# Order of the first three shared products in a fused graph and mixture-of-experts layer

## The chip, the cores and the metric

The kernel runs on one core of a Trainium2 chip. The metric is the device time of one execution in microseconds; before the change it is 2880.34 us, the median of three runs (2879.47 to 2881.34).

The engines have these names: PE is TensorE (matrix products into PSUM banks), DVE is VectorE, ACT is ScalarE, POOL is GpSimd, SP is SyncE, which issues the loads of weights. They run their own programs side by side and wait for each other by semaphores.

## The reference

For 625 tokens of width 1024 the layer computes, in float32:

```
xn = layernorm(x)
x  = x + graph_attention(xn) + linear_attention(xn)
x  = x + ffn(layernorm(x))
ffn(t) = (silu(t @ sg) * (t @ su)) @ sd                    # shared, 1024 -> 8192 -> 1024
       + sum over the two chosen of 8 experts, at most 97 tokens each:
         w * (silu(g @ rg) * (g @ ru)) @ rd                # routed, 1024 -> 4096 -> 1024
```

The weights of the shared part (sg, su, sd) and of the experts (rg, ru, rd) are read once, about 500 MB.

## The kernel before

The graph and the attention parts take the first 470 us; then 32 steps of about 75 us do the feed-forward part. A step is an expert e (0 to 7) and a quarter q (0 to 3) of its inner width, and with it 256 columns of the shared inner width. Step 0 has an order of its own (`FIRST`), step 31 another (`LAST`); the 30 between them (`STEP`) run the code that is changed. In seven of these q is 0: there an expert begins, and its tokens, gathered from memory into `xg`, are transposed by PE (`turn_expert`), copied from PSUM by ACT (`tokens_hi`) and split by DVE (`tokens_lo`, which raises `xgT_ready`).

Weights arrive as 128x1024 blocks of float32 in a ring of raw buffers. Each block is used as a unit u: ACT casts it to a rounded high part (`hi(u)`, `c_hi`), DVE subtracts that from the block (`lo(u)`, `c_lo`), and PE forms each product of two numbers by three matmuls (`three`: high by high, high by low, low by high). High and low parts have a ring of seven places, and `hi(u)` waits until PE has used unit u-7. PE waits for `lo(u)` by `split(u)`.

The first seven units of a step serve the two shared up projections, gate and up, as a 2x2 block product done with seven products instead of eight. Their names are F_A11, F_S3, F_S2, F_A12, F_S1, F_A22, F_S4, for the units 0 to 6. Those with S take sums of raw blocks that DVE makes in place (`factor_sum`): S3 out of A11 and A21, then S2 out of S3, and so on. `product(j, i)` is the product i for the half j of the unit's columns, 12 matmuls into one PSUM bank; both halves use the same unit. The banks of half 0 are 2 to 5, those of half 1 are 6, 7, 0 and 1. Products with S3 and A11 start an empty bank; the later ones go on top of a copy of an earlier one, which ACT makes (`seed`). `keep_e7(j)` is ACT's copy of the S3 product out of its bank.

Bank 6 also gathers the routed down projection of the step before. So `product(1, F_A11)` waits for `rd_added`: ACT must first have copied this bank to `eout` (`routed_out(0)`), and it may do so only when PE is through with the last routed unit. In ACT's order, which is written out by hand, `routed_out(0)` stands behind `hi(3)`. The end of a step on PE is: the transposes of the second half of the routed inner rows (`turn_inner(1)`), then six units of `routed_down`, then the next step's `product(0, F_A11)`.

In the trace all matmuls of `three` have the lines L2164, L2167 and L2168. ACT: casts L736 (shared units) and L871, `routed_out` L960, seeds L890, `keep_e7` L895, tokens L972, `turned_hi` L915. DVE: low parts L1260 and L1630, sums for S3 L1243, S2 L1247, S1 L1250, S4 L1253, `turned_lo` L1739, `tokens_lo` L1745. PE's transposes are L2215 (`turn_inner`) and L2226 (`turn_expert`).

Of the kernel before, what the change touches and what calls it, by code (L numbers as in the profile page):

```python
# [103 lines left out]
F_A11, F_S3, F_S2, F_A12, F_S1, F_A22, F_S4 = range(NPROD)  # L104
# [64 lines left out]
def count(e, q, per_step, n):  # L169

    return e * (Q * per_step) + (q * per_step + n)
# [10 lines left out]
def build(nc, x, src, dst, W, a, w_qkv, w_out, b_out, router_w, rg, ru, rd, sg, su, sd, out):  # L182
# [3 lines left out]
    def sem(name):  # L186
        if name not in sems:
            sems[name] = ctx.enter_context(nc.semaphore(name))
        return sems[name]
# [280 lines left out]
    def raw_at_(q, b):  # L470

        return raw[(q * BLK + b) % RAW]

    def raw_sem(q, b):
        return sem(f"raw_in{(q * BLK + b) % RAW}")

    def raw_full(e, q, b):

        return e * (16 * Q * BLK // RAW) + 16 * ((q * BLK + b) // RAW + 1)
# [187 lines left out]
    def _(act):  # L667
# [57 lines left out]
        def factor_hi(e, q, order, i):  # L725
            u = order.at(i)
            r = order.raw(u)
            if SUM_BEFORE[i]:
                act.wait_ge(sem("sums"), count(e, q, 4, SUM_BEFORE[i]))
            else:  # L730
                act.wait_ge(raw_sem(q, r), raw_full(e, q, r))
            act.wait_ge(sem("unit_used"), count(e, q, U, u + 1 - RING + USED0))
            if order is FIRST and i in (F_A22, F_S4):
                act.wait_ge(sem("sums_y"), 4)
                act.wait_ge(sem("block_lo"), 2)
            nc.scalar.copy(c_hi[u % RING][:], raw_at_(q, r)[:]).then_inc(sem("hi_done"), 1)  # L736
# [66 lines left out]
        for n in range(2 * PAIRS):  # L803
            g, i = divmod(n, 4)
# [56 lines left out]
        def step(e, q, order=STEP):  # L861
            def hi(u):

                if order.shared(u):
                    return factor_hi(e, q, order, order.seq[u - order.s])
                r = order.raw(u)
                act.wait_ge(raw_sem(q, r), raw_full(e, q, r))
                act.wait_ge(sem("unit_used"), count(e, q, U, u + 1 - RING + USED0))
                if order is STEP and u in (order.sd + 2, order.sd + 3):
                    act.wait_ge(sem("down_sums"), count(e, q, 4, 2 * (u - order.sd - 1)))  # L870
                nc.scalar.copy(c_hi[u % RING][:], raw_at_(q, r)[:]).then_inc(  # L871
                    sem("hi_done"), 1 + (U - order.units) * (u == order.units - 1))
# [6 lines left out]
            def product_done(j, i):  # L879
                if j == 0:  # L880
                    act.wait_ge(sem("s_half"), count(e, q, NPROD, order.at(i) - order.s + 1))
                else:
                    act.wait_ge(sem("unit_used"), count(e, q, U, order.at(i) + 1 + USED0))
# [8 lines left out]
            def keep_e7(j):  # L892

                product_done(j, F_S3)
                nc.scalar.copy(s_up[:, j, 0:HW], PS[order.banks[j][3]][:, 0:HW]).then_inc(sem("seeded"), 1)  # L895
# [162 lines left out]
                tokens_hi(0)  # L1058
            hi(5)
            hi(6)  # L1060
            hi(7)
            keep_e7(0)
            if q == 0:
                tokens_hi(1)
            keep_e7(1)
# [54 lines left out]
        for q in range(Q):  # L1120
            step(0, q, FIRST if q == 0 else STEP)
        with act.Fori(1, E - 1) as e:
            for q in range(Q):
                step(e, q)
        for q in range(Q):
            step(E - 1, q, LAST if q == Q - 1 else STEP)
# [780 lines left out]
    def _(pe):  # L1907
# [132 lines left out]
        for n in range(2 * PAIRS):  # L2040
            g, i = G_Q + n // 4, n % 4
# [115 lines left out]
        def step(e, q, order=STEP):  # L2157
            def split(u):

                pe.wait_ge(sem("lo_done"), count(e, q, U, U + u + 1))  # L2160

            def three(out_, l_hi, l_lo, r_hi, r_lo, first, last, used=False, skip=False):

                m = MM(out_, l_hi, r_hi, start=first, stop=False, skip_group_check=skip)  # L2164
                if used:
                    m.then_inc(sem("unit_used"), used)
                MM(out_, l_hi, r_lo, start=False, stop=False, skip_group_check=skip)  # L2167
                return MM(out_, l_lo, r_hi, start=False, stop=last, skip_group_check=skip)  # L2168
# [16 lines left out]
            def product(j, i):  # L2185

                a, c, b, d = order.banks[j]
                bank = (a, d, a, b, a, c, d)
                after = {F_S2: TO_B, F_A12: TO_B, F_S1: TO_C, F_A22: TO_C, F_S4: TO_D}
                u = order.at(i)  # L2190
                t = FACTOR_TOK[i]
                split(u)
                if order is FIRST and j == 0:
                    pe.wait_ge(sem("block_lo"), BLK_LO.index(t) + 1)
                if i == F_S3 and order is FIRST:
                    pe.wait_ge(sem("silu_done"), count(e, q, 6, order.silus(1, 0)))
                elif i == F_S3 and j == 1 and order is LAST:
                    pe.wait_ge(sem("silu_done"), count(e, q, 6, order.silus(0, 1)))
                if i in after:
                    pe.wait_ge(sem("seeded"), count(e, q, 8, order.seeded(j, after[i])))  # L2200
                for k in range(4):
                    col = slice(k * 256 + j * P, k * 256 + (j + 1) * P)
                    m = three(PS[bank[i]][:, 0:HW], c_hi[u % RING][:, col], c_lo[u % RING][:, col],
                              tok_hi[t][:, k, :], tok_lo[t][:, k, :], k == 0 and i not in after, k == 3,
                              skip=(i in after))
                m.then_inc(sem("unit_used" if j else "s_half"), 1)
# [12 lines left out]
            def turn_expert(halves=(0, 1)):  # L2219

                pe.wait_ge(sem("xg_in"), e * 16 + 16)
                pe.wait_ge(sem("tlo_done"), count(e, q, 2, ONE))
                for half in halves:
                    for k in range(4):
                        c = (4 * half + k) * P
                        m = TR(PS[order.x_bank[half]][:, k * CAP:(k + 1) * CAP], xg[0:CAP, c:c + P], ident[0:CAP, 0:CAP])  # L2226
                    m.then_inc(sem("xgT_ps"), 1)
# [162 lines left out]
                return  # L2390

            product(0, F_A11)
            pe.wait_ge(sem("rd_added"), count(e, q, 2, 1))
            product(1, F_A11)
            if q == 0:
                turn_expert((0,))
                product(0, F_S3)
                product(0, F_S2)
                pe.wait_ge(sem("xgT_ready"), e * 2 + 1)
                turn_expert((1,))  # L2400
                product(0, F_A12)
                pe.wait_ge(sem("xgT_ready"), e * 2 + 2)
                for i in (F_S3, F_S2, F_A12):
                    product(1, i)
            else:
                for i in (F_S3, F_S2, F_A12):
                    product(0, i)
                    product(1, i)
            for i in (F_S1, F_A22, F_S4):
# [22 lines left out]
        for q in range(Q):  # L2432
            step(0, q, FIRST if q == 0 else STEP)
        for e in range(1, E - 1):
            for q in range(Q):
                step(e, q)
        for q in range(Q):
            step(E - 1, q, LAST if q == Q - 1 else STEP)
# [32 lines left out]
```

## Time and profile before

| what | value |
|---|---|
| median of three runs | 2880.34 us |
| profiled execution | 2882.55 us, of which the span is 2880.9 us |
| PE busy | 2801.1 us (97%) |
| DVE busy | 2364.3 us (82%) |
| ACT busy | 1783.4 us (62%) |
| mean granted clock of PE | 0.984 of full speed |
| mean DMA rate | 191 GB/s |

Busy time is the time in which at least one instruction of the engine runs. For PE it grows when the granted clock falls, so a busy PE isn't always a fast one. The clock has its own column in the views of single stretches.

### The profile page before, as it was taken

To read this page: it belongs to the slowest core of one execution; us is meant where nothing else is said; L and a number is where in the kernel's file an instruction comes from. 1 tells how busy PE (TensorE), PEld (TensorE's weight loads), DVE (VectorE), ACT (ScalarE), POOL (GpSimd) and SP (SyncE) were. 2 spreads that over 40 slices of the span, in tenths; PEclk is the share of its full clock that TensorE was granted. 3 is DMA by queue.
4 is the path that set the end of the run, shared out by engine and by line. 5 is a ranking of instruction groups with operands and counts; after the bars stand their busy time and mean duration, and the time that the engine had idled before them with its cause. 6 is when DMAs were issued, how large, how long until landed. Compare 5 with 4: busy or idle time off the path is not lost.

```text
span 2880.9 us, 42107 instructions
## 1 busy us (share of the span) xinstructions
PE 2801.1 (97%) x14756; PEld 2330.2 (81%) x14756; DVE 2364.3 (82%) x2957; ACT 1783.4 (62%) x2509; POOL 62.6 (2%) x74
## 2 busy tenths in 40 slices
PE   9999999999999999999999999999999999999998
PEld 8878898877777778887888877887888877777777
DVE  8857258988888888888888888888888888888888
ACT  7632224666666666666666666666666666666673
POOL 0010000000000000000000000000000000000001
PEclk9999999999999999999999999999999999999999
DMA  3011123766666666665666666667666666666676
GB/s 112 30 66 59 59 74 95 247 218 213 216 210 206 212 225 219 219 205 198 221 205 207 208 222 214 206 211 225 219 210 214 225 213 214 216 215 206 208 263 223
DMA packets 270286, 549.14 MB, mean 191 GB/s; under 512 B 16673, under 2 KB 82465, under 8 KB 269927
## 3 DMA queue, kind: packets, MB, share of 16 engines
q1 hardware_dynamic: 265954, 532.11, 56.2%
q0 software_dynamic: 3936, 14.06, 1.6%
q8 instruction: 118, 1.93, 0.3%
q14 instruction: 116, 0.95, 0.1%
q10 hardware_dynamic: 162, 0.08, 0.0%
HBM read 537.49 MB, written 8.70 MB: 190 GB/s over the span
## 4 chain that ended last, share of the span: by engine, by line
PE 78%; DVE 14%; issue 3%; ACT 3%; DMA 2%; ACTq 0%; SPq 0%; DVEq 0%
PE ps L2164 21%; PE ps L2167 21%; PE ps L2168 21%; DVE c_lo L1630 5%; PE ps L1928 3%; PE ps L1965 2%; PE ps L1967 2%; PE ps L1966 2%; DVE c_lo L1260 2%; ACT c_hi L736 1%; DVE raw L1247 1%; DVE raw L1243 1%; DMA raw<-in_L_ffn_su 1%; PE ps L2215 1%; PE ps L2056 1%
## 5 line engine op out<-in xcount | busy, mean ns | idle before, releaser
L1630 DVE TENSOR_TENSOR c_lo<-raw,c_hi 128x1024 fp32r<-128x1024 f32 x892 | 1055.4, 1219 | 246.3 <-ACT c_hi L871 245.3
L871 ACT CAST c_hi<-raw 128x1024 fp32r<-128x1024 f32 x892 | 903.3, 1048 | 226.0 <-PE ps L2168 83.0
L2164 PE MATMUL ps<-tok_hi,c_hi 128*128 128x314 f32 x1792 | 573.1, 320 | 62.9 <-ACT eout L960 62.5
L2168 PE MATMUL ps<-tok_hi,c_lo 128*128 128x314 f32 x1792 | 567.8, 317 | 0.0
L2167 PE MATMUL ps<-tok_lo,c_hi 128*128 128x314 f32 x1792 | 567.8, 317 | 0.0
L2164 PEld LDWEIGHTS ps<-tok_hi,c_hi 128*128 128x128 f32 x1792 | 353.7, 197 | 74.3 <-ACT eout L960 70.3
L2164 PE MATMUL ps<-c_hi,xgT_hi 128*97 128x512 f32 x1024 | 404.6, 395 | 0.0
L2168 PE MATMUL ps<-c_hi,xgT_lo 128*97 128x512 f32 x1024 | 403.1, 394 | 0.0
L2167 PE MATMUL ps<-c_lo,xgT_hi 128*97 128x512 f32 x1024 | 403.0, 394 | 0.0
L736 ACT CAST c_hi<-raw 128x1024 fp32r<-128x1024 f32 x224 | 228.7, 1049 | 215.0 <-DVE raw L1243 108.9
L2167 PEld LDWEIGHTS ps<-tok_lo,c_hi 128*128 128x128 f32 x1792 | 353.8, 197 | 1.4
L2168 PEld LDWEIGHTS ps<-tok_hi,c_lo 128*128 128x128 f32 x1792 | 352.8, 197 | 0.0
L1260 DVE TENSOR_TENSOR c_lo<-raw,c_hi 128x1024 fp32r<-128x1024 f32 x224 | 268.5, 1220 | 31.1 <-ACT c_hi L736 29.5
L2168 PEld LDWEIGHTS ps<-c_hi,xgT_lo 128*97 128x97 f32 x1024 | 166.1, 162 | 70.6
L2167 PEld LDWEIGHTS ps<-c_lo,xgT_hi 128*97 128x97 f32 x1024 | 166.3, 162 | 66.4
L2164 PEld LDWEIGHTS ps<-c_hi,xgT_hi 128*97 128x97 f32 x1024 | 166.3, 162 | 65.8
L2164 PE MATMUL ps<-c_hi,hT_hi 128*97 128x512 f32 x512 | 203.3, 397 | 0.0
L2168 PE MATMUL ps<-c_hi,hT_lo 128*97 128x512 f32 x512 | 201.6, 394 | 0.0
L2167 PE MATMUL ps<-c_lo,hT_hi 128*97 128x512 f32 x512 | 200.8, 392 | 0.0
L890 ACT COPY ps<-ps 128x314 f32<-128x314 f32 x192 | 78.8, 410 | 128.9 <-PE ps L2168 127.2
L1729 DVE TENSOR_TENSOR resid<-ps,resid 125x512 f32<-125x512 f32 x240 | 148.6, 681 | 0.0
L2164 PE MATMUL ps<-c_hi,sh_hi 128*125 128x512 f32 x340 | 134.4, 395 | 0.1
(286 smaller groups left out, 4083.7 us busy)
## 6 DMA issues: line engine op xcount, KB each, us to landing
raw<-in_L_ffn_rg SPq DMA_DIRECT2D x256, 512.0 KB, 5.0
raw<-in_L_ffn_ru SPq DMA_DIRECT2D x256, 512.0 KB, 4.1
raw<-in_L_ffn_rd SPq DMA_DIRECT2D x256, 512.0 KB, 5.0
raw<-in_L_ffn_sg SPq DMA_DIRECT2D x64, 512.0 KB, 5.9
raw<-in_L_ffn_su SPq DMA_DIRECT2D x64, 512.0 KB, 6.5
raw<-in_L_ffn_sd SPq DMA_DIRECT2D x64, 512.0 KB, 6.8
wl<-in_L_mix_w_qkv SPq DMA_DIRECT2D x6, 2048.0 KB, 8.0
wl<-in_L_gnn_W SPq DMA_DIRECT2D x2, 2048.0 KB, 21.9
```

Source lines behind the costliest of these rows:

```text
L736: nc.scalar.copy(c_hi[u % RING][:], raw_at_(q, r)[:]).then_inc(sem("hi_done"), 1)
L871: nc.scalar.copy(c_hi[u % RING][:], raw_at_(q, r)[:]).then_inc(sem("hi_done"), 1 + (U - order.units) * (u == order.units - 1))
L890: nc.scalar.copy(PS[to][:, 0:HW], PS[a][:, 0:HW]).then_inc(sem("seeded"), 1)
L1260: V.tensor_tensor(c_lo[u % RING][:], raw_at_(q, r)[:], c_hi[u % RING][:].bitcast(F32), ALU.subtract).then_inc(sem("lo_done"), 1)
L1630: V.tensor_tensor(c_lo[u % RING][:], raw_at_(q, r)[:], c_hi[u % RING][:].bitcast(F32), ALU.subtract).then_inc(sem("lo_done"), 1 + (U - ord ...
L1729: V.tensor_tensor(r, PS[bank][0:TP, :], r, ALU.add).then_inc(sem("sd_added"), n)
L1928: m = MM(PS[dt][0:TP, 0:SC], oh_d[slot(gr, c)][:, dt * TP:(dt + 1) * TP], oh_s[slot(gr, c)][:, 0:SC], start=(c == 0), stop=(c == EG - 1))
L1965: MM(ps, l_hi[:, k, ts], hi[:, i, :], start=(k == 0), stop=False)
L1966: MM(ps, l_hi[:, k, ts], lo[:, i, :], start=False, stop=False)
L2164: m = MM(out_, l_hi, r_hi, start=first, stop=False, skip_group_check=skip)
L2167: MM(out_, l_hi, r_lo, start=False, stop=False, skip_group_check=skip)
L2168: return MM(out_, l_lo, r_hi, start=False, stop=last, skip_group_check=skip)
```

## The change

PE: in every ordinary step `product(0, F_S3)` comes directly behind `product(0, F_A11)`, ahead of the wait for `rd_added` and of `product(1, F_A11)`. In the steps with q not 0 the sequence A11/0, A11/1, S3/0, S3/1, S2/0, ... becomes A11/0, S3/0, A11/1, S3/1, S2/0, ... In those with q=0 the sequence A11/0, A11/1, transposes, S3/0, S2/0, transposes, A12/0, S3/1, ... becomes A11/0, S3/0, A11/1, transposes, S2/0, transposes, A12/0, S3/1, ... ACT: `keep_e7(0)` goes ahead of `hi(7)` instead of behind it.

```diff
--- before.py
+++ after.py
@@ -1058,8 +1058,8 @@
                 tokens_hi(0)
             hi(5)
             hi(6)
+            keep_e7(0)
             hi(7)
-            keep_e7(0)
             if q == 0:
                 tokens_hi(1)
             keep_e7(1)
@@ -2390,11 +2390,11 @@
                 return
 
             product(0, F_A11)
+            product(0, F_S3)
             pe.wait_ge(sem("rd_added"), count(e, q, 2, 1))
             product(1, F_A11)
             if q == 0:
                 turn_expert((0,))
-                product(0, F_S3)
                 product(0, F_S2)
                 pe.wait_ge(sem("xgT_ready"), e * 2 + 1)
                 turn_expert((1,))
@@ -2403,7 +2403,8 @@
                 for i in (F_S3, F_S2, F_A12):
                     product(1, i)
             else:
-                for i in (F_S3, F_S2, F_A12):
+                product(1, F_S3)
+                for i in (F_S2, F_A12):
                     product(0, i)
                     product(1, i)
             for i in (F_S1, F_A22, F_S4):
```

## Rows read from the trace of the kernel before

**Rows 1.** The page: span, and busy time of each engine.

```profile
span 2880.9 us, 42107 instructions
...
PE 2801.1 (97%) x14756; PEld 2330.2 (81%) x14756; DVE 2364.3 (82%) x2957; ACT 1783.4 (62%) x2509; POOL 62.6 (2%) x74
```

**Rows 2.** Waits of PE: for whom, us in total, times, longest.

```profile
PE ps L2164 <- ACT eout L960: 62.5, 30, 3.2
...
PE ps L2164 <- DVE xgT_lo L1745: 0.4, 1, 0.4
```

**Rows 3.** PE timeline, step with q=2: start us, us, what [idle before].

```profile
1516.07 0.50 PE L2215 MATMUL ps<-ident,r_h 97*128 97x97 f32 x4
...
1524.71 0.31 PE L2164 MATMUL ps<-tok_hi,c_hi 128*128 128x314 f32 x1
...
1526.32 0.31 PE L2168 MATMUL ps<-tok_hi,c_lo 128*128 128x314 f32 x1
1528.61 0.42 PE L2164 MATMUL ps<-tok_hi,c_hi 128*128 128x314 f32 x1 [1.99 <-ACT eout L960]
```

**Rows 4.** Timeline of DVE, same stretch.

```profile
1517.12 0.56 DVE L1739 TENSOR_TENSOR hT_lo<-ps,hT_hi 128x388 fp32r<-128x388 f32 x1 [0.62 <-ACT hT_hi L915]
...
1521.01 1.22 DVE L1243 TENSOR_TENSOR raw<-raw,raw 128x1024 f32<-128x1024 f32 x1
1522.14 2.50 DVE L1260 TENSOR_TENSOR c_lo<-raw,c_hi 128x1024 fp32r<-128x1024 f32 x2
1524.75 1.23 DVE L1247 TENSOR_TENSOR raw<-raw,raw 128x1024 f32<-128x1024 f32 x1
```

**Rows 5.** Timeline of ACT, same stretch.

```profile
1526.08 1.99 ACT L736 CAST c_hi<-raw 128x1024 fp32r<-128x1024 f32 x2 [2.69 <-DVE raw L1247]
1527.98 1.07 ACT L960 COPY eout<-ps 97x512 f32<-97x512 f32 x2
1528.93 0.44 ACT L890 COPY ps<-ps 128x314 f32<-128x314 f32 x1
```

**Rows 6.** Stretches, PE alone: length, busy, PEclk (granted clock), DMA share, GB/s.

```profile
1526.62:1528.61 1.99, 0.00 (x2) 1.00 0.00 0
1529.37:1532.78 3.41, 3.41 (x15) 0.50 0.00 0
553.00:559.00 6.00, 5.60 (x37) 1.00 0.16 60
```

**Rows 7.** A11_1 to S1_0, q not 0, low clock: first of 17, sum.

```profile
702.12:715.96 13.84, 13.84 (x84) 0.88 0.59 204
...
sum 234.98, PE 234.97; mean PE 13.82
```

**Rows 8.** The same stretch in the five steps at full clock: one, sum.

```profile
1001.86:1014.14 12.28, 12.28 (x84) 1.00 0.58 186
...
sum 61.48, PE 61.47; mean PE 12.29
```

**Rows 9.** The same stretch in the seven steps with q=0: sum.

```profile
sum 105.43, PE 105.05; mean PE 15.01
```

**Rows 10.** Timeline of ACT in a step with q=0.

```profile
1979.76 1.05 ACT L736 CAST c_hi<-raw 128x1024 fp32r<-128x1024 f32 x1
...
1982.64 0.48 ACT L972 CAST xgT_hi<-ps 128x388 fp32r<-128x388 f32 x1 [0.24 <-PE ps L2226]
1983.02 2.00 ACT L736 CAST c_hi<-raw 128x1024 fp32r<-128x1024 f32 x2
```

**Rows 11.** Timeline of DVE in that step.

```profile
1984.11 1.22 DVE L1260 TENSOR_TENSOR c_lo<-raw,c_hi 128x1024 fp32r<-128x1024 f32 x1 [1.66 <-ACT c_hi L736]
1985.25 0.56 DVE L1745 TENSOR_TENSOR xgT_lo<-ps,xgT_hi 128x388 fp32r<-128x388 f32 x1
...
1987.99 0.56 DVE L1745 TENSOR_TENSOR xgT_lo<-ps,xgT_hi 128x388 fp32r<-128x388 f32 x1
```

**Rows 12.** One whole step at full clock, all engines.

```profile
629.03:702.12 73.09, 71.25 (x375) 58.49 (x375) 63.26 (x71) 49.70 (x69) 0.00 (x0) 1.00 0.65 216
```

## Prediction

> **What bounds the kernel now.** I read the page's head first: TensorE (PE) is busy for 2801.1 of 2880.9 us [rows 1], so its 80 us of idle time and the speed at which it runs are what there is to win. Second, the waits of PE: 62.5 us of the idle time are 30 waits of one kind, a matmul of a product that waits for ScalarE's copy of the routed accumulator into `eout` [rows 2]. Thirty is the number of ordinary steps, the one wait a step that `rd_added` makes. Third, the timelines around one such wait, in a step with q=2. PE turns the last routed rows at 1516.07, goes on without a pause to the last matmul of `product(0, F_A11)` at 1526.32, and starts `product(1, F_A11)` at 1528.61 after 1.99 us of idleness [rows 3]. VectorE (DVE) explains the lateness. After that turn it is fed at once (`hT_lo` at 1517.12, after 0.62 us of waiting for it) and then has no pause: three low parts, the sum for S3, the low parts of units 0 and 1 (until 1524.64), the sum for S2 (until 1525.98) [rows 4]. ScalarE takes `hi(2)` and `hi(3)` only when that sum is there (1526.08), and the copy to `eout` stands behind them: 1527.98 [rows 5]. So `product(1, F_A11)` starts 12.54 us after the turn whatever PE does in between, and PE has only 10.55 us of work for it.
>
> Fourth, the clock. During the 1.99 us the granted clock is still full; from 0.76 us after the restart it is 0.50 (1.2 of 2.4 GHz) for 3.41 us [rows 6]. The price is seen in the stretch from the start of `product(1, F_A11)` to the start of `product(0, F_S1)`. In the 17 steps with q not 0 and a clock below 1.00 it takes 234.98/17 = 13.82 us [rows 7], in the five with clock 1.00 it takes 61.48/5 = 12.30 [rows 8]. So a low stretch costs 1.52 us. In the seven steps with q=0, which hold two transposes of tokens besides, it takes 105.43/7 = 15.06, all at a lowered clock [rows 9].
>
> **The change, part by part.** Nothing is added or removed: the same matmuls, casts and DMAs, in another order on PE and, by one place, on ScalarE. No DMA issue is moved past anything.
>
> *`product(0, F_S3)` ahead of the wait.* Twelve matmuls from 1524.71 to 1526.32 give (1526.32-1524.71)/11 = 0.146 each, 1.75 a product [rows 3]. PE can issue the next product at 1526.47. Its unit is 1, whose low part is ready at 1524.64 [rows 4], 1.8 us before. It fills 1.75 us of idle time and leaves 1.99-1.75 = 0.24. It can't push the wait back: from the end of `lo(1)` to the restart there are 1528.61-1524.64 = 3.97 us, as the sum, two casts and the copy all follow on it, and the product needs 1.75, or 3.5 at half the clock. Its bank was last read by `turned_lo(1)`, which PE had to wait for before the fifth routed down unit. `product(1, F_A11)` therefore starts when it did, and every product behind it comes one product earlier.
>
> *The low clock.* It follows the idle time: the one step whose wait was only 0.40 us (at 555.95) shows clock 1.00 in the 6 us around it, 5.60 of them busy [rows 6]. With about 0.2 us left in the steps with q not 0, I take no low stretch there. That saves 1.52 more in 17 steps.
>
> The Trainium skill speaks against this term: "TensorE: Matmul & The Clock Gate", section "Why this matters for your kernels", warns only of idle gaps about as long as the longest of the 30 waits (3.2 us, rows 2). By that rule the low stretches would have another cause and stay; that is rival B. The trace does not agree, since 1.99 us are followed by 0.50 in rows 6.
>
> *Sum for q not 0.* The stretch falls to 12.30-1.75 = 10.55. Gain: 17 x (13.82-10.55) = 55.6; 5 x 1.75 = 8.8; in the step with the 0.40 us wait just 0.4. Together 64.8 us. Behind the stretch all is paced by PE: DVE waits for ScalarE's casts, these for ring places that PE frees, and so moves along. On the way nothing is late: after the restart ScalarE has four casts and four copies in front of `hi(8)`, about 4 x 1.0+4 x 0.42 = 5.7 us by the durations in rows 5, so the low parts of S1, A22 and S4 are there by about 7 us, and PE wants the first of them at 10.55. The seeds that S2 waits for are copied at 1528.93 (0.32 after the restart, [rows 5]) and when `product(1, F_A11)` has drained, some 2 us after it; PE comes to them 3.5 and 5.25 us after it.
>
> *Steps with q=0.* Here the transposes of the tokens have to be copied by ScalarE and split by DVE before `turn_expert((1,))` and `product(1, F_S3)` may start. Before, two products stood in front of the first of these waits, now one. I set `product(1, F_A11)` at 0 and take spacings of ScalarE and DVE from the step at 1979.09 [rows 10, 11]. `hi(4)` starts at 0.67 and takes 1.05; the seed of `product(1, F_A11)` starts when that product has drained, 1.95 (full clock), and takes 0.41; the transposes are over at 2.25; the copy of the first token half runs 2.30 to 2.78, `hi(5)` from 2.68, its low part from 3.77 (1.09 behind the cast's start, as at 1983.02 and 1984.11), `tokens_lo(0)` 4.91 to 5.47. PE has done with transposes and `product(0, F_S2)` at 3.77, so it waits about 1.75 us and turns the second half at 5.5. ScalarE copies that at 6.05 to 6.53, DVE splits it behind `lo(7)` at 7.65 to 8.2. PE reaches `product(1, F_S3)` at 7.55 and waits 0.7. Three products on, `product(0, F_S1)` starts at 13.5 instead of 15.06: 1.55 us, 7 x 1.55 = 10.9. The bounds: with no token wait at all it would be 6 products and 0.6 for transposes, 11.1, gain 28; with both token waits ending where they end now in rows 11 (DVE done at 1985.81 and 1988.55, so 6.7 and 9.5), 14.7, gain 2.5. A low stretch after the 1.75 us idleness costs 1.52, of which the second wait hides 0.7, so 0.8 a step, 5.6 in all. I take 10 us, near the walk by rows. Of the idle time ahead of `product(1, F_A11)` in these steps (up to 3.2) 1.75 go as well, but that is the same gain: the start is unchanged.
>
> *`keep_e7(0)` ahead of `hi(7)`.* The copy of 0.42 us comes before a cast whose low part PE needs over 10 us later: nothing. Without that cover it would be 0.42 x 30 = 13 us. What it waits for is ready earlier than now.
>
> **Sum.** 64.8+10 = 75 us. The profiled execution took 2882.55 (span 2880.9), 2.2 above the median of the runs, so 2807.6 by it and 2880.3-75 = 2805 against the median. I say 2806.
>
> **Rivals.**
> A, the forecast: both terms, 2800 to 2814 with the token steps' bounds that I believe. Chance 0.75.
> B, the low clock stays in the steps that have it, because something else lowers it or the token waits and 0.24 us still suffice. Then 22 x 1.75+0.4 = 39, token steps some 4: 43 us, 2837. For it: five steps have no low stretch although PE idled before them too, the one at 1001.86 among them [rows 8], so idleness alone doesn't decide. Against: no low stretch in the step with 0.40. Chance 0.12, partly so included.
> C, another engine sets the pace once PE is shorter: DVE is busy for 63.26 of 73.09 us of a step [rows 12] and has next to no pause before the turn. If 73.09 were its floor, only the clock comes back: 17 x 1.52 = 26 us, 2854. Against: the waits of 0.62 us just before `hT_lo` show it waiting for PE's work [rows 4]. Chance 0.07.
> D, slower: the token chain. PE's cover in front of it goes from two products to one; if the gather or ScalarE's queue is later than in my walk and each such wait brings a low stretch, the stretch in the seven steps takes 16.6 instead of 15.06, +11 us, 2891. It decides the sum only if the other 23 steps give under 0.5 us each, that is with C at its fullest. Chance 0.03.
> E, the change does nothing, as something in front of `product(0, F_S3)` holds it until ScalarE's copy: 2880. Chance 0.03.
>
> **How the numbers follow.** 2806 is A. The range, 2798 to 2840, holds A and B; C, D and E lie outside. A measurement of this kernel tells 0.2% (6 us) from no change. Faster is A, B and C, 0.94; same 0.03; slower 0.03.
>
> **What would show it.** Right: PE's waits for `eout` fall from 62.5 to about 12 us, about 0.2 each in steps with q not 0; clock 1.00 in the stretches of rows 7, and 10.55 us for each; a new wait for `xgT_lo` of some 1.7 and 0.7 us in seven steps; 12.5 us from the turn to `product(1, F_A11)` as before; 71.3 us a step. Wrong: a clock of 0.50 after each step's start, or waits of PE for `c_lo` behind the products (C).

## The result, and the profile after

The changed kernel takes 2810.02 us (median of four runs, 2807.42 to 2810.77) against 2880.84 us before: the ratio is 0.9751, 95% interval 0.9734 to 0.9767. The forecast was 2806, with 2798 to 2840 as its range.

The page of the changed kernel; its profiled execution took 2810.77 us.

```profile
span 2809.2 us, 42107 instructions
...
PE 2763.9 (98%) x14756; PEld 2290.7 (82%) x14756; DVE 2363.4 (84%) x2957; ACT 1779.7 (63%) x2509; POOL 61.5 (2%) x74
```

As many instructions, 71.8 us less than the profiled execution before. PE's busy time fell by 37.2 us (2801.1 to 2763.9, [rows 1]) although it does the same matmuls: that part is the clock. The rest, 34.5 of the 71.7 us by which the span is shorter, is idle time.

Waits of PE in the changed kernel (for whom: us in total, times, longest):

```profile
PE ps L2226 <- DVE xgT_lo L1745: 10.4, 7, 1.5
PE ps L2164 <- ACT eout L960: 10.3, 24, 1.4
...
PE ps L2164 <- DVE c_lo L1260: 4.0, 3, 2.1
PE ps L2164 <- DVE xgT_lo L1745: 2.9, 7, 0.4
```

The wait for `eout` is down from 62.5 to 10.3 us [rows 2]. The first row is new, as forecast: the second transposes of the tokens, seven times, 1.49 us each. The third wasn't in the forecast.

The same stretch of the same step as in [rows 3], on PE:

```profile
1487.07 0.50 PE L2215 MATMUL ps<-ident,r_h 97*128 97x97 f32 x4
...
1497.45 0.30 PE L2164 MATMUL ps<-tok_hi,c_hi 128*128 128x314 f32 x1
...
1499.61 0.41 PE L2164 MATMUL ps<-tok_hi,c_hi 128*128 128x314 f32 x1 [0.24 <-ACT eout L960]
```

Between the turn of the routed rows and the restart there are 12.54 us, as before. The second product now begins at 1497.45 and takes 1.75 us of the pause, of which 0.24 us is left.

What the restart waits for, on DVE (one row) and ACT (two rows), with the distances of [rows 4, 5]:

```profile
1495.74 1.22 DVE L1247 TENSOR_TENSOR raw<-raw,raw 128x1024 f32<-128x1024 f32 x1
...
1497.07 2.00 ACT L736 CAST c_hi<-raw 128x1024 fp32r<-128x1024 f32 x2 [2.69 <-DVE raw L1247]
1498.98 1.07 ACT L960 COPY eout<-ps 97x512 f32<-97x512 f32 x2
```

The sum for S2 ends at 1496.96, ScalarE takes `hi(2)` and `hi(3)` at 1497.07, and `eout` comes 1.91 us later, as before (1527.98-1526.08 = 1.90). PE's new order changes none of these distances.

The stretch from the second A11 product to the first S1 product, for the 17 steps of [rows 7] (the first, and their sum), the five of [rows 8] (sum) and the seven of [rows 9] (one, sum). Columns: from and to, length, PE busy, granted clock, DMA share, GB/s.

```profile
698.97:709.53 10.56, 10.56 (x72) 1.00 0.50 157
...
sum 179.54, PE 179.51; mean PE 10.56
...
sum 52.80, PE 52.80; mean PE 10.56
...
770.45:784.13 13.68, 11.78 (x80) 1.00 0.65 219
...
sum 95.79, PE 82.48; mean PE 11.78
```

The 17 take 10.56 us each instead of 13.82, the five 10.56 instead of 12.30, the seven 13.68 instead of 15.06. The clock is 1.00 in all 30 steps. That is 55.4+8.7+9.6 = 73.7 us.

In a step with q=0, the transposes of both token halves and `product(1, F_S3)` on PE:

```profile
1936.64 0.50 PE L2226 MATMUL ps<-ident,xg 97*128 97x97 f32 x4
...
1940.39 0.56 PE L2226 MATMUL ps<-ident,xg 97*128 97x97 f32 x4 [1.49 <-DVE xgT_lo L1745]
...
1943.12 0.41 PE L2164 MATMUL ps<-tok_hi,c_hi 128*128 128x314 f32 x1 [0.41 <-DVE xgT_lo L1745]
```

At the starts of the experts 2 to 6 something else is late: DVE's sum for S3 waits for its load for 2.99, 1.54, 2.94, 0.11 and 0.91 us (in the kernel before 1.33, 0, 1.01, 0.93 and 0.27). At e=4, SyncE's queue issues the rows on L543 below, the last of the old step's loads and then the first of the new one's; the sum waits for the first `su`:

```profile
1608.93 14.48 SPq L543 DMA_DIRECT2D raw<-in_L_ffn_rd  x8
1630.44 0.39 SPq L543 DMA_DIRECT2D raw<-in_L_ffn_sg  x1
1631.02 2.67 SPq L543 DMA_DIRECT2D raw<-in_L_ffn_su  x2
...
1637.97 1.22 DVE L1243 TENSOR_TENSOR raw<-raw,raw 128x1024 f32<-128x1024 f32 x1 [2.94 <-DMA raw<-in_L_ffn_su]
```

The restart of this step comes 15.56 us after the turn instead of 12.54. There, and most of all at e=2, PE has to wait for the low part of unit 0 too, the third row of its waits. This looks like the sign of rival C, but it is another thing: DVE has nothing to do there until the load has landed.

### The profile page after: what moved, and what is told of

It reads as the page before. It is cut to its first block, busy times and chain, and to the rows that moved or that the text cites. A ratio compares the mean times of both kernels' runs of the same rounds, so it can differ in the third digit from the quotient of the medians.

```text
span 2809.2 us, 42107 instructions
## 1 busy us (share of the span) xinstructions
PE 2763.9 (98%) x14756; PEld 2290.7 (82%) x14756; DVE 2363.4 (84%) x2957; ACT 1779.7 (63%) x2509; POOL 61.5 (2%) x74
## 4 chain that ended last, share of the span: by engine, by line
PE 76%; DVE 15%; issue 4%; ACT 3%; DMA 1%; ACTq 0%; SPq 0%; DVEq 0%
PE ps L2164 20%; PE ps L2168 20%; PE ps L2167 20%; DVE c_lo L1630 6%; PE ps L1928 3%; PE ps L1965 2%; PE ps L1967 2%; PE ps L1966 2%; DVE c_lo L1260 2%; ACT c_hi L736 2%; DVE raw L1247 1%; DVE raw L1243 1%; DMA raw<-in_L_ffn_su 1%; PE ps L2215 1%; PE ps L2056 1%
## 5 line engine op out<-in xcount | busy, mean ns | idle before, releaser
L2164 PE MATMUL ps<-tok_hi,c_hi 128*128 128x314 f32 x1792 | 556.8, 311 | 17.6 <-ACT eout L960 10.3
L2168 PE MATMUL ps<-tok_hi,c_lo 128*128 128x314 f32 x1792 | 551.6, 308 | 0.0
L2167 PE MATMUL ps<-tok_lo,c_hi 128*128 128x314 f32 x1792 | 551.4, 308 | 0.0
L2164 PEld LDWEIGHTS ps<-tok_hi,c_hi 128*128 128x128 f32 x1792 | 338.9, 189 | 30.0 <-ACT eout L960 18.1
L2167 PEld LDWEIGHTS ps<-tok_lo,c_hi 128*128 128x128 f32 x1792 | 339.3, 189 | 1.3
L2168 PEld LDWEIGHTS ps<-tok_hi,c_lo 128*128 128x128 f32 x1792 | 337.7, 188 | 0.0
L2168 PE MATMUL ps<-c_hi,sh_lo 128*125 128x512 f32 x340 | 134.1, 394 | 0.0
```

## The experiments

Each run was compared with runs of the kernel before on the same chip; there were three chips. The medians were 2878.19 us for the two halves of the change, the whole useless product and the written-out loop; 2877.49 for the half useless product, the early copy to `eout` by itself, the tokens' earlier path and all edits together; 2880.03 for the early copy on the changed kernel and the two runs on ScalarE's part. Ratios are to them, with 95% intervals. Where two runs come from different chips, their ratios are compared, not their times; the changed kernel has 0.9751 and, on the third chip, 0.9759.

### The two halves of the change by themselves

Edit of the first (q not 0 alone), on PE; ScalarE's swap is bound to `if q:` in the same way:

```diff
             product(0, F_A11)
-            product(0, F_S3)
+            if q:
+                product(0, F_S3)
             pe.wait_ge(sem("rd_added"), count(e, q, 2, 1))
...
                 turn_expert((0,))
+                product(0, F_S3)
                 product(0, F_S2)
```

> The new order on PE and ScalarE in the 23 ordinary steps with q not 0 alone; the seven with q=0 keep the old one. Theory (each half of the change acts on its own steps, through the product that covers the wait and through the clock): stretches of 10.56 us at clock 1.00 in the 23 steps, about 62 us less than before, near 2817 us, and low clock left in most of the seven steps with q=0. Rival (the low clock belongs to the kernel as a whole, or returns when only some steps are mended): low stretches of 3.41 us stay in steps with q not 0 too, gain about 39 us, near 2842.

Measured: 2814.8 us, ratio 0.9775 (0.9758 to 0.9791), 63.4 us less. Stretches of the 22 steps with q not 0 other than step 1 (sum), and of the first and the last of the seven with q=0:

```profile
sum 232.33, PE 232.31; mean PE 10.56
...
771.50:786.25 14.75, 14.75 (x93) 0.88 0.60 202
...
2523.96:2537.64 13.68, 13.31 (x92) 1.00 0.67 222
```

232.33/22 = 10.56 us, all at full clock. Six of the seven steps with q=0, which kept their order, still run at a lowered clock. The clock is a matter of the single step.

The other half binds the same edits to `if q == 0`.

> The new order in the seven steps with q=0 alone. Theory: stretch from the second A11 product to the first S1 product 13.68 us instead of 15.06, with new waits for the tokens of 1.5 and 0.4 us and clock 1.00 there; gain 7 x 1.4 = 10 us less up to 4 us that PE loses again at the starts of experts, so 2871 to 2875. Rival (the token waits cost what the product gives): no gain, 2880. The other 23 steps keep 13.8 us and their low clock.

Measured: 2868.76 us, ratio 0.9967 (0.9955 to 0.9980), 9.4 us less, as expected. One step with q=3, then one of the seven with q=0 and their sum:

```profile
702.22:716.03 13.81, 13.81 (x84) 0.88 0.61 210
...
776.95:790.64 13.69, 11.79 (x81) 1.00 0.65 220
...
sum 95.82, PE 82.53; mean PE 11.79
```

The seven take 95.82/7 = 13.69 us. Of the other 22 steps (without step 1) 17 have a low stretch and five don't, as in the kernel before, after the same pauses of 1.84 to 1.99 us; but they are not the same five, only the first is spared in both. The halves add up: 63.4+9.4 = 72.8 us, and 0.9775 x 0.9967 = 0.9743 against 0.9751.

### Useless work in the place of the wait

```diff
+            product(0, F_A11, done=False)
             product(0, F_A11)
             pe.wait_ge(sem("rd_added"), count(e, q, 2, 1))
```

With `done=False` the product raises no semaphore; the second one starts the bank afresh and gives the same values.

> The kernel before, in which PE forms the product A11 of half 0 twice in each ordinary step, the second time over the first, so that the wait is filled with useless work and no product is moved. Theory (the low clock comes from the idle time ahead of it): no low stretch, 12.30 us from A11 of half 1 to S1 in the 17 steps instead of 13.82, about 13.5 instead of 15.06 in the seven with q=0; gain 26+10 = 36 us, near 2844. Rival (something else lowers the clock, idleness does not matter): the low stretches stay, 2880 us.

Measured: 2847.69 us, ratio 0.9897 (0.9881 to 0.9914), 30.5 us less, where 36 were expected. Against the profiled execution of before, on which the 36 us rest, it is 35.5 us (2882.55 to 2847.07). The nine runs of the kernel before on this chip had a mean granted clock of 0.986 to 0.988, the profiled one 0.984, so fewer of their steps may have been slow; they left no trace that would show it. 360 matmuls are added and the kernel is faster. The 17 steps (one, sum), and the sum of the seven with q=0:

```profile
702.39:714.68 12.29, 12.29 (x85) 1.00 0.58 195
...
sum 209.29, PE 209.27; mean PE 12.31
...
sum 95.77, PE 93.18; mean PE 13.31
```

209.29/17 = 12.31 us at clock 1.00, where the kernel before has 13.82 at 0.88. The low clock comes from the idle time, and what it costs is 1.5 us a step. Rival B falls.

The Trainium skill, "TensorE: Matmul & The Clock Gate", section "Why this matters for your kernels", warns only of idle gaps over about 3 us. The trace does not agree: 18 of the 24 gaps that lowered the clock in the kernel before were 1.84 to 1.99 us.

The last row says something that the forecast had not seen. The seven steps with q=0 take 95.77 us in this kernel, with PE's old order, and 95.79 in the changed one. There the moved product buys nothing beyond the clock that the filled pause keeps. The chain of the tokens sets the time in both: what PE saves in front of `turn_expert((1,))` it waits for there.

### Half of the wait filled

The edit is the one above with six matmuls in place of twelve (`n=2`, over the inner blocks k).

> The kernel before, in which PE forms only the first half (6 of 12 matmuls) of the product A11 of half 0 a second time, so that about 1.1 us of the 1.99 us wait stay idle. This looks at the clock between 0.24 us (no low stretch) and 1.99 us (low in most steps). Theory (a shorter idle time is enough): clock 1.00 in the stretches with q not 0, about the time of the kernel with the whole product twice, near 2848 us. Rival (any idle time of about 1 us lowers the clock in some steps): low stretches of 3.41 us in more than five of the thirty steps, over 2855 us.

Measured, one run: 2852.12 us. The stretches of the 22 steps (sum); then in two steps with q=0 the idle time ahead of the restart and the time behind it:

```profile
sum 270.95, PE 270.92; mean PE 12.31
...
1363.90:1365.94 2.04, 0.00 (x0) 1.00 1.06 390
1366.21:1369.62 3.41, 3.41 (x17) 0.50 0.85 291
...
1662.04:1664.27 2.23, 0.00 (x1) 1.00 1.02 378
1664.27:1668.00 3.73, 3.73 (x27) 1.00 0.44 144
```

The 22 steps idle for 0.98 to 1.19 us and take 270.95/22 = 12.32 us, so none has a low stretch. Where the idle time is over 2 us, at four starts of experts, three show one (two more like the first pair are not copied: 2.11 and 2.25 us) and one, 2.23 us, does not. So the rival's five steps weren't reached. At e=2 the pause was 1.74 us and the clock stayed full.

Over the thirty steps of all the traces kept, variants included, none of the 95 pauses of 0.9 to 1.78 us lowered the clock, and 58 of the 77 pauses of 1.83 us and more did. No low stretch in these steps came without such a pause. What spares the others is open.

### The copy to `eout` ahead of the casts

```diff
             hi(1)
-            hi(2)
-            hi(3)
             routed_out(0)
             routed_out(1)
+            hi(2)
+            hi(3)
```

This is the kernel before with PE's old order.

> The kernel before with PE's old order, in which ScalarE copies the routed accumulator to eout ahead of hi(2) and hi(3) instead of behind them, in the 2.7 us in which it waits for the sum for S2 anyway. Theory (the wait of PE comes from the order of ScalarE's queue, not from PE's order): the wait for eout falls to 0 in all thirty steps, the low stretches go, a step with q not 0 takes 71.1 us against 71.47 in the changed kernel, and in those with q=0 the tokens come earlier too; 2785 to 2800 us, less than the changed kernel. Rival (the copies delay hi(2), and with it S2 or the seeds): new waits for c_lo or seeds eat it, 2810 or more.

Measured: 2797.31 us, ratio 0.9719 (0.9703 to 0.9735), less than the changed kernel. In a step with q=2 the copy runs while ScalarE would wait for the sum, and the casts are ready right behind it:

```profile
1488.41 1.07 ACT L960 COPY eout<-ps 97x512 f32<-97x512 f32 x2 [1.52 <-PE ps L2168]
1489.58 2.00 ACT L736 CAST c_hi<-raw 128x1024 fp32r<-128x1024 f32 x2
```

Waits of PE, of which none is for `eout`:

```profile
PE ps L2226 <- DVE xgT_lo L1745: 13.5, 7, 2.5
...
PE ps L2164 <- DVE c_lo L1260: 5.0, 3, 2.1
```

So the wait was made by two casts in front of the copy in ScalarE's order. The change hides it behind a product, this edit takes it away. The steps with q=0 gain less than I expected: PE waits for the tokens in all seven, up to 2.5 us. At e=5, on PE, ACT, DVE and PE again, and then the stretch behind the same wait at e=2:

```profile
1924.90 0.50 PE L2226 MATMUL ps<-ident,xg 97*128 97x97 f32 x4
1927.43 0.48 ACT L972 CAST xgT_hi<-ps 128x388 fp32r<-128x388 f32 x1
1930.82 0.55 DVE L1745 TENSOR_TENSOR xgT_lo<-ps,xgT_hi 128x388 fp32r<-128x388 f32 x1
1931.43 0.91 PE L2226 MATMUL ps<-ident,xg 97*128 97x97 f32 x4 [2.52 <-DVE xgT_lo L1745]
...
1063.86:1067.27 3.41, 3.41 (x15) 0.50 0.71 216
```

The gathered tokens are there in time, as PE transposes the first half without a wait. ScalarE's copy of it comes 2.0 us after the transposes, behind casts and seeds, and DVE's split 2.9 us after that copy, behind sums and low parts, neither engine being idle just before. So it is again the order of two queues; in the last run, which takes the tokens earlier in both, none of these waits is over 0.6 us. Nor did all low stretches go, as I had expected: three of these waits (e=2, 4 and 5) and one for a low part (e=6), 2.01 to 2.54 us long, brought one each, that at e=5 of 6.83 us; the mean clock is 0.997.

The same edit on the changed kernel:

> The changed kernel, with ScalarE's copy to eout ahead of hi(2) as in the run with PE's old order. Theory (the product moved by the change now has no wait to cover; what is left of it goes, 0.24 us in steps with q not 0 and up to 1.4 in those with q=0): 5 to 12 us below the changed kernel, 2796 to 2805, and within 5 us of PE's old order with the same edit (0.972 of the kernel before). Rival (the two edits add up): under 2790 us.

Measured: 2799.9 us, ratio 0.9725 (0.9709 to 0.9741), beside 2808.8 for the changed kernel on that chip: 9 us less, and as fast as the edit alone. The two answer to one wait and do not add up. Here too three pauses, of 2.52, 2.52 and 3.14 us, lowered the clock. Its waits of PE:

```profile
PE ps L2226 <- DVE xgT_lo L1745: 14.4, 7, 2.6
...
PE ps L2164 <- DVE c_lo L1260: 4.0, 4, 3.1
```

### ScalarE's part of the change, and the changed kernel again

> The changed kernel's order on PE with ScalarE's old order (keep_e7(0) behind hi(7)). Theory (the place of this 0.42 us copy is free, as the low part of unit 7 is ready over 10 us before PE needs it): same time as the changed kernel within 2 us, beside it on this chip. Rival (the new place of the copy is part of the gain): 3 us or more slower.

> The changed kernel itself on the same chip, as the measure for the two beside it: about 0.975 of the kernel before, 2807 to 2810 us.

Measured: 2807.94 us (0.9755, 0.9739 to 0.9771) with `keep_e7(0)` behind `hi(7)` as before, 2808.8 us (0.9759, 0.9741 to 0.9777) for the changed kernel. The place of the copy makes no difference that can be measured.

### The starts of the experts

```diff
-        with sp.Fori(1, E - 1) as e:
+        for e in range(1, E - 1):
             for q in range(Q):
                 step(e, q)
```

> The changed kernel with SyncE's loop over the experts 1 to 6 written out, so that its queue of loads has no jump back; all else the same. Theory (the 3 to 4 us that are missing from the predicted gain lie at the starts of experts 2 to 6, where the first load of shared weights is issued 13 to 15 us before the second A11 product instead of 18): the load comes at 18 us there too, those five steps start 12.54 us after the turn of the routed rows, 9 us less in all, near 2801 us. Rival (ScalarE's own loop, or the time that the loads take in the DMA engines, holds those steps): within 3 us of 2810.

Measured: 2801.9 us, ratio 0.9734 (0.9717 to 0.9750). By the ratios this is 5 to 7 us below the changed kernel, where 9 were expected, and the two intervals overlap; the spans of the two profiled executions differ by 7.1 us (2809.2 and 2802.1). What the edit does is seen in the trace. SyncE's loads around the start of e=4 and DVE's sum, then PE's wait for `eout`:

```profile
1605.39 14.32 SPq L543 DMA_DIRECT2D raw<-in_L_ffn_rd  x8
1620.52 0.38 SPq L543 DMA_DIRECT2D raw<-in_L_ffn_sg  x1
1621.65 1.97 SPq L543 DMA_DIRECT2D raw<-in_L_ffn_su  x2
...
1631.40 1.22 DVE L1243 TENSOR_TENSOR raw<-raw,raw 128x1024 f32<-128x1024 f32 x1
```

```profile
PE ps L2164 <- ACT eout L960: 6.6, 24, 1.0
```

From the end of the last `rd` issue to the first `sg` issue there are 0.81 us, in the changed kernel 7.03. In the changed kernel this distance is 6.3 to 7.2 us at the five starts that lie behind a jump back, and 0.8 to 1.0 us at the other steps of the loop; in this run it is 0.8 us everywhere. The `sg` load is issued 5.9 us ahead of the turn instead of 0.4 us behind it, and no DMA wait stands ahead of the sum. PE's waits for `eout` fall from 10.3 to 6.6 us and the 4.0 us for low parts go. In three of the five starts (e=3, 4 and 5) the restart comes 12.54 us after the turn, at e=2 and e=6 13.30 and 12.80. So the queue of loads was held up where its loop jumps back. How much of the 5.4 to 6.3 us is the jump itself, and how much what the loop works out ahead of its first load, was not separated. Why e=2 keeps 0.76 us was not tried.

### The tokens' path earlier, and all together

PE makes the first transposes ahead of the wait; ScalarE copies the halves ahead of `hi(4)` and behind `hi(6)`; DVE:

```diff
+                if tokens:
+                    tokens_lo(0)
                 lo(order.s + F_S1)
                 lo(order.s + F_A22)
                 if tokens:
-                    tokens_lo(0)
+                    tokens_lo(1)
                 lo(order.s + F_S4)
```

> The changed kernel, and in the seven steps with q=0 the path of the tokens earlier on three engines: PE makes the first four transposes ahead of the wait for the copy to eout, ScalarE copies the halves ahead of hi(4) and behind hi(6), VectorE splits them ahead of the low parts of S1 and of S4. Theory (in these steps the chain of the tokens sets the time, S3 of half 1 waits for it until 8.35 us): both waits for xgT_lo go, S1 of half 0 starts at about 10.9 us instead of 13.68, 7 x 2.8 = 20 us less than the changed kernel, near 2790 us. Rival (ScalarE or VectorE is late with the shared units when the tokens go first): the waits turn into waits for c_lo and the gain is under 5 us, 2805 to 2810.

Measured: 2790.54 us, ratio 0.9697 (0.9681 to 0.9713), by the ratios 16 to 18 us below the changed kernel, where 20 were expected. All waits for `xgT_lo` are gone; at e=2 a wait of 1.99 us for a low part still brings one low stretch. In a step with q=0 both transposes run without a pause behind them, and the only idle time left is the one for `eout`:

```profile
1921.01 0.50 PE L2226 MATMUL ps<-ident,xg 97*128 97x97 f32 x4
1922.21 0.41 PE L2164 MATMUL ps<-tok_hi,c_hi 128*128 128x314 f32 x1 [0.69 <-ACT eout L960]
...
1925.79 0.50 PE L2226 MATMUL ps<-ident,xg 97*128 97x97 f32 x4
```

With the loop written out and the copy to `eout` early as well:

> The changed kernel with the three further edits together: copy to eout ahead of hi(2), path of the tokens earlier as above, SyncE's loop written out. Theory: each acts on its own wait, 5 to 8 us, about 20 us and 8 us below the changed kernel's 2810, so 2775 to 2780 us, and PE idles for under 5 us in the thirty steps. Rival (the three gains are one and the same idle time): not under 2790 us.

Measured: 2777.28 us, ratio 0.9651 (0.9635 to 0.9667), by the ratios 29 to 31 us below the changed kernel; the three edits by themselves gave 9, 16 to 18 and 5 to 7. PE over nearly all of the 30 steps, in the changed kernel and in this one:

```profile
550.00:2725.00 2175.00, 2146.97 (x11282) 1.00 0.67 221
```

```profile
550.00:2690.00 2140.00, 2138.03 (x11287) 1.00 0.68 225
```

28.0 us of idle time became 2.0. The gains come from different waits and nearly add up, and the thirty steps are now bound by PE's own work at full clock.

## Why the prediction was right

It held at almost every step of its sum.

- *What bounds.* The wait comes from the queue of ScalarE. The edit of ScalarE's order alone removed all 30 waits.
- *`product(0, F_S3)` fills the pause and delays nothing.* 0.24 us left where 0.24 were forecast, the restart 12.54 us after the turn in the steps with q not 0.
- *The low clock goes.* In all 30 steps. The duplicate product shows the size: 13.82 to 12.31 us, 1.51 where 1.52 was set.
- *q not 0, 64.8 us.* 55.4+8.7 = 64.1 measured in the stretches of the profiled executions, and 63.4 by the run with these steps alone. For step 1 I had 0.4 us.
- *q=0, 10 us.* The stretches gave 9.6, the run with these steps alone 9.4, and the walk's 13.5 us is 13.68; its two token waits of 1.75 and 0.7 us measured 1.49 and 0.41. The size was right and one reason was not: I booked the moved product as a gain and the token waits as its cost. The kernel with the useless product has the same 13.68 us, so cover and wait cancel, and the whole gain in these stretches is that of the clock.
- *`keep_e7(0)`, nothing.* Nothing.
- *The term that was missing.* The stretches give 73.7 us, the profiled executions differ by 71.8. I took the time from the turn to the restart as fixed. It is in the steps with q not 0, but for one (13.22 to 12.54 us, at e=3 and q=1). At starts of experts it hangs on loads that are issued behind a jump in SyncE's queue, and it wasn't 12.54 us there in the kernel before either. It grew from 13.96 to 15.99 us at e=2, from 13.33 to 14.16 at e=3, from 13.73 to 15.56 at e=4 and from 12.89 to 13.53 at e=6, and fell from 13.56 to 12.74 at e=5, 3.8 us in all over the steps; under 2 us the other way are spread over the rest. The hold-up behind the jump is in the kernel before too, 6.0 to 6.8 us; at e=4 the load is issued 0.2 us later behind the turn than before, and the sum begins 6.95 us after that issue instead of 5.22. Why the load took longer was not tested. That the forecast misses by only 4 us owes something to these two remainders having opposite signs.

Of the rivals, C (DVE sets the pace) has its answer in the last run: a step with q not 0 takes 70.97 us there (2336.84 to 2407.81 us), with DVE's same work of some 63. D never came near in the changed kernel: the token waits of 1.49 and 0.42 us lowered no clock. Its mechanism is real, though: in the two kernels with the early copy to `eout` eight such waits were 2.14 to 2.55 us long, and five of them brought a low stretch. E would have shown as a start of the product later than 1497.45.

## What to carry to other kernels

A wait at the head of a repeated step can cost more than its idle time: here 24 of 29 pauses of about 2 us and more brought slow matmuls with them, 1.5 us in a typical step, so look at the granted clock behind every pause and count both. Ask first what stands in front of the releasing instruction in its own queue. To move two casts behind it was worth more (0.972 of the kernel before) than to find work for the one who waits (0.975). And where a filled pause meets a second chain (the tokens here), a duplicate of useless work tells how much of the gain is the clock's and how much is the order's.

## What the runs showed of the hardware

- Idle times of PE of 0.98 to 1.19 us never lowered its clock (22 steps of the kernel with the half useless product), nor did seven token waits of 1.49 us in the changed kernel; 1.84 to 3.2 us did in 24 of the 29 such steps before. Of four pauses of 2.04 to 2.25 us one stayed at full clock, so the length of the pause alone doesn't settle it.
- A low stretch of 3.41 us at clock 0.50 (1.2 of 2.4 GHz) cost 1.5 us. In the kernel before it began up to 1.6 us after the restart in 22 of 24 steps, so the slow matmuls are not those next to it alone. In the other two (e=2 and 3, pauses of 3.11 and 2.78 us) the clock fell while PE still idled, 1.1 and 0.7 us ahead of the restart, and stayed low for 6.83 us.
- Where a loop jumps back on SyncE, the first load of the next pass was issued 6.0 to 7.2 us after the end of the issue before it, against 0.8 to 1.0 us at the loop's other steps and 0.8 us with the loop written out, with no compute engine at fault.
